# Three buffers instead of four for the expert tiles' inputs and outputs, in a two-layer transformer kernel

## What is computed

```python
x = x + _L0_attn_ref(_layernorm(x, axis=-1), ...)
x = x + _L0_ffn_ref(_layernorm(x, axis=-1), ...)
x = x + _L1_attn_ref(_layernorm(x, axis=-1), ...)
x = x + _L1_ffn_ref(_layernorm(x, axis=-1), ...)
```

## Time and profile before

| what | value |
|---|---|
| time, median of 3 runs | 3438.32 us (3438.31 to 3441.68) |
| the profiled execution's own time | 3441.68 us |
| its span, first to last instruction | 3439.8 us |
| expert stage, first load to last scatter issued | 1376.5 to 1598.2 us |
| busy over the whole span | PE 90%, DVE 73%, ACT 67%, POOL 45% |
| mean granted TensorE clock | 0.945 |

### The profile page before, as it was taken

How to read it: one execution, slowest core, us unless ns; L and a number is a source line. 1 busy time by engine, 2 the same in 40 slices (tenths; PEclk the granted TensorE clock), 3 DMA queues, 4 the chain that set the end, 5 groups by cost and what they waited for, 6 DMA issues and landing times. The chain is left out here.

```text
span 3439.8 us, 73149 instructions
## 1 busy us (share of the span) xinstructions
PE 3110.3 (90%) x22770; PEld 1708.7 (50%) x22770; DVE 2501.7 (73%) x7023; ACT 2299.8 (67%) x3127; POOL 1533.6 (45%) x1807
## 2 busy tenths in 40 slices
PE   6999996799999885994499999999999999999979
PEld 2555553455555553883244444444444444444456
DVE  4666654888888872664688888888888888888754
ACT  4877772465655553443688888888888888888722
POOL 3454442345555534576434444444444444444433
PEclk8999996899999997997699999999999999999989
DMA  4444542322222212563200000000000000000001
GB/s 102 117 107 102 118 115 61 73 57 58 61 64 66 65 43 48 170 175 110 58 0 4 6 2 7 0 9 0 9 0 3 6 0 9 0 9 0 0 16 34
DMA packets 173144, 162.18 MB, mean 47 GB/s; under 512 B 18276, under 2 KB 156735, under 8 KB 172830
## 3 DMA queue, kind: packets, MB, share of 16 engines
q1 hardware_dynamic: 163838, 142.35, 17.1%
q0 software_dynamic: 9088, 16.88, 1.5%
HBM read 92.40 MB, written 68.52 MB: 47 GB/s over the span
## 5 line engine op out<-in xcount | busy, mean ns | idle before, releaser
L2759 POOL TENSOR_TENSOR lb_y<-lb_ao,XC 128x512 f32<-128x512 f32 x128 | 163.1, 1274 | 801.7 <-ACT lb_ao L2706 801.7
L2598 PE MATMUL lb_H<-lb_x,lb_w 128*128 (+1 forms) x1024 | 513.7, 604 | 0.5 <-issue 0.5
L547 ACT ACTIVATE ga_PT<-ga_S 128x1024 f32<-128x1024 f32 (+1 forms) x384 | 336.6, 881 | 262.7 <-PE ga_S L374 262.4
L2607 PE MATMUL lb_FF<-lb_h,lb_w 128*128 128x512 f32 x1024 | 460.3, 592 | 0.0
L2713 ACT ACTIVATE lb_h<-lb_H,lb_prm 128x512 f32<-128x512 f32 x512 | 351.7, 687 | 99.4 <-PE lb_H L2598 84.4
L2805 DVE TENSOR_SCALAR lb_z<-lb_M,lb_mv,lb_rstd 128x128 f32<-128x128 f32 x1024 | 349.9, 404 | 32.9 <-POOL lb_rstd L2750 27.7
L2607 PEld LDWEIGHTS lb_FF<-lb_h,lb_w 128*128 128x128 f32 x1024 | 194.6, 190 | 244.9 <-issue 215.4
L2750 POOL TENSOR_TENSOR lb_rstd<-lb_rstd,half 128x4 f32<-128x4 f32 x256 | 259.2, 1012 | 36.9 <-issue 0.2
L2797 DVE BATCH_NORM_STATS2 lb_stats<-lb_M 128x6 f32<-128x128 f32 x1024 | 228.3, 286 | 29.5 <-PE lb_M L2580 18.0
L2598 PEld LDWEIGHTS lb_H<-lb_x,lb_w 128*128 128x128 f32 x1024 | 174.0, 190 | 132.2 <-issue 122.8
L1522 POOL TENSOR_SCALAR_AFFINE_SELECT da_PT<-da_PT 128x1024 f32<-128x1024 f32 x128 | 145.9, 1145 | 201.1 <-ACT da_PT L1452 201.1
(11 more groups left out here) (335 smaller groups left out, 7185.9 us busy)
## 6 DMA issues: line engine op xcount, KB each, us to landing
moe_w<-experts_dram SPq DMA_DIRECT2D x39, 384.0 KB, 3.3
da_qT<-da_stq SPq DMA_DIRECT2D x64, 192.0 KB, 4.2
da_kT<-da_stk SPq DMA_DIRECT2D x64, 192.0 KB, 5.1
ga_qT<-ga_stq SPq DMA_DIRECT2D x32, 384.0 KB, 6.1
moe_x<-moe_xs SPq DMA_DIRECT2D x39, 258.0 KB, 3.7
tc_g<-moe_ys SPq DMA_DIRECT2D x32, 256.0 KB, 3.5
da_stq<-da_parts SPq DMA_DIRECT2D x16, 384.0 KB, 2.4
da_stk<-da_parts SPq DMA_DIRECT2D x16, 384.0 KB, 3.0
```

The lines of the kernel that those rows point to most:

```text
L547: act.activation(PT[:, n % RING, :, lo:hi], score_banks(u)[:, :, 0:hi - lo], ACT.Exp, scale=SCALE).then_inc(probs, 1)
L2598: pe.matmul(H[:, k % 2, :], w1[:, k, :], x1_of(i), start=True, stop=True).then_inc(h_filled, 1)
L2607: pe.matmul(FF[:, :], w2[:, k, :], h[:, k, :], start=(k == 0), stop=(k == KC - 1)).then_inc(ff_filled, 1)
```

## The change

The counts of buffers XR (for x and w) and YR (for y and the destinations) go from 4 to 3. All else follows from these two numbers: how many tiles are loaded at the start, which tile a load has to wait for, how far `address` may run ahead of the scatters, and the size of the four tensors.

```diff
@@ -1783,8 +1783,8 @@
 
     F = 256
     FC = F // P
-    XR = 4
-    YR = 4
+    XR = 3
+    YR = 3
 
     own = []
     with ExitStack() as ctx:
```

## The result

| | median of the runs | runs |
|---|---|---|
| before | 3440.0 us | 4, 3438.31 to 3442.75 |
| changed | 3535.9 us | 4, 3532.49 to 3541.84 |
| ratio | 1.028 | 95% interval 1.0262 to 1.0298 |

The changed kernel is 95.9 us slower; the prediction said 99.9 us and 3538 us.

The account below looks back on a forecast made before the run. The prediction took the w load's undivided round trip of 8.0 us as the period, replacing POOL's 5.2 us a tile; 36 trips plus the end made the stage 99.9 us longer: 3438.3 + 99.9 = 3538 us, range 3518 to 3566.

Parts of the forecast that it names:

- The bound: Expert stage: POOL's 5.2 us a tile sets the end before; with three buffers the w load's undivided round trip does.
- which take releases which load: w(j+XR) is issued after take(j); its round trip has two periods with four buffers, one with three.
- The trip: From take through w load and copy_w to the next take: 1.43 + 3.3 + 3.23 = 7.96 us, taken as 8.0.
- the sum of 99.9: Expert stage's end: 36 round trips of 8.0 us, then POOL's last tiles, ending at 1698.1 instead of 1598.17.
- The estimate of 2.9 us for the load: Alternative price for the 384 KB w load from the skill's fit: period 7.6 us, 3524 us in all.
- YR costs nothing: In address, waiting for scatters of tile j-3: 7.9 us against two periods of 16 us, so no wait, no cost.
- TensorE is early: In each tile TensorE finishes 3.9 us before its down is wanted and idles 3.0 us.
- the clock rival: TensorE's clock falls to 0.50 throughout, period 10.0 us, 72 us more, 3610 us; chance 0.06.
- ACT's wait: ACT's wait for w ahead of copy_w: some 5.7 us a tile, about 205 us in all instead of 65.9.
- The end: Stage's end: POOL finishes three tiles 19.6 us after copy_w(38); last scatter starts about 10 us behind last take.
- The start: Stage's start: take(0) stays at 1393.76; dropping the fourth tile's initial loads changes nothing.
- POOL's waits: POOL's scatters wait for take about 2.8 us a tile, some 100 us in all.

Follow-up runs that it names:

- x3y4: The changed kernel with YR back at 4 (XR = 3): 3538.48 us against 3445.72 us of the kernel before beside it, ratio 1.0266.
- down_gate: The changed kernel (XR = YR = 3) with the w load waiting for the tile's down matmuls instead of the copy behind them: 3469.05 us, ratio 1.0065 to the kernel before.
- split3: The changed kernel with w in two loads, gate and up released after rest_of_w, down as in the changed kernel: 3446.32 us, ratio 1.0004 to the kernel before.
- dbl3: The changed kernel (XR = YR = 3) with every later w load done twice, the second after the first has landed: 3683.23 us.
- dbl4: The kernel before (XR = YR = 4) with every later w load done twice, run two times: 1.0020 and 1.0004 of the kernel before beside it.
- x4y3: The kernel before with YR = 3 and XR still 4: 3442.85 us, ratio 0.9997 to the kernel before.
- base_again: The kernel before, unchanged, run and profiled again on another chip: 3530.78 us.
- x5y4: The kernel before with a fifth input buffer (XR = 5, YR = 4): ratio 1.0003, beside a kernel before of 3529.82 us.
- split3b: split3 with the gate and up load issued one tile further ahead, run two times: 1.0024 and 1.0016 of the kernel before beside it.

## Why the prediction was right

- *The bound, and which take releases which load.* Right, and shown: x3y4 puts the loss on XR, down_gate and split3 take three quarters and all of it back through the release of the load alone, and dbl3 against dbl4 shows the trip paid once a tile with three buffers and covered with four.
- *The trip.* Worked out 7.96 us, rounded to 8.0; measured 7.88 on average in the changed kernel and 7.90 in x3y4. In the trip shown above 1.43 to the issue was 1.43, and 3.23 from copy_w to take was 3.20; if these hold for the others, the load's mean is what is left of 7.88, 3.25 where I took 3.3. The rounding and the load together are 36 x 0.12 = 4.3 us, and the sum of 99.9 is 4.0 above the measured 95.9.
- The estimate of 2.9 us for the load from the fit in the Trainium skill ("DMA: Bandwidth & Descriptors", Anatomy of one DMA) would have given 3524 us, below all timed runs; the row of this queue was the better price.
- *YR costs nothing.* Right for the time (x4y3). Wrong in a detail: alone, beside XR = 4, it does make address wait, 54.1 us. I had compared the trip with two whole periods, and left out that VectorE, ahead of POOL, runs into the ring whatever its length. The wait takes the place of POOL's backlog and is free.
- *TensorE is early and the clock rival.* TensorE idles 2.6 us in the tile shown and (50 - 36.44) / 50 x 7.9 = 2.1 a tile on average (I had 3.0). The clock was not at 1.00 as I had expected. Windows of the changed kernel:

```profile
1422.00:1470.00 48.00, 35.63 (x198) 29.17 (x197) 19.31 (x36) 13.08 (x24) 26.48 (x26) 0.93 0.39 118
...
1520.00:1570.00 50.00, 36.44 (x197) 30.04 (x198) 21.64 (x41) 13.80 (x26) 24.83 (x25) 0.92 0.35 106
```

  It dips and comes back. The burst at 1520.82 begins at a granted clock of 1.00 after 2.61 us of idle time; the clock is 0.50 from 1522 to 1524 and 1.00 again from 1525, and the first four matmuls are busy for 1.53 us in place of 1.17. A mean of 0.92 costs nothing, since TensorE has 3.9 us to spare, as said. The Trainium skill ("TensorE: Matmul & The Clock Gate", HAM oscillation) describes a kernel in which every burst behind a DMA wait starts low. Here most bursts run at 1.00 throughout, and in the one shown the fall comes after its start.
- *ACT's wait.* Forecast about 205 us, measured 232.3; I had left out its wait for the first tile, 26.7 us before and 25.6 after. POOL's waits: about 100 forecast, 125.3 - 27.3 = 98.
- *The end.* From the start of take(36) to the end of the last scatter 16.3 us by my sum, 16.6 measured. Two errors nearly cancel in it, which is luck: from take to its first scatter the sum has 1.0 us, and it is 1.57 in the earlier trace rows (1393.76 to 1395.33) and 1.51 at 1703.37; and twelve scatters take 15.1 us, where the sum has 15.3. The last scatter starts 8.3 us behind the last take (9.9 in x3y4), where I had said about 10. The start: take(0) stands 17.3 us behind the first load before and 17.4 after.

## What to carry to other kernels

A ring of n buffers gives a load's round trip fewer periods than n. Subtract those that the consumer's own order uses up, here two: going from four to three halved the cover instead of taking a quarter. Add the whole trip up, from the release through the issue and the landing to the next release, and divide it by that number; as long as it is below the slowest engine's pace a buffer less costs nothing, and beyond that each microsecond is paid on every tile. Before buying a buffer, look at what releases it: a release at the last reader, or two loads for parts that are read last at different times, gave back three quarters and all of the loss with three buffers. And a wait that grows (address in x4y3, ACT in split3) is no loss where the engine that sets the pace is still fed.

## What the runs showed of the hardware that was not expected

The same kernel took 3440 us beside some runs and 3531 us beside others, each steady to about 0.4%. The profiles of the second kind in which the load of w does not set the pace (base_again, x5y4, dbl4, split3b) have idle times of ACT and DVE ("remote", "issue"; up to 5.4 us in base_again) that no instruction of the program explains. Most of them lie in the expert stage, which took 280.1 us in place of 221.7. The two kinds went with the chip in these runs; that it is the chip, and not something else that differed between the times of the runs, was not tested. What these engines wait for was not found. That w or x land later does not explain it: in x5y4 the waits for both (29.1 us of ACT for w, 26.8 us of TensorE for x) were those of the start alone, and the stage took 288.2 us. What can be said is that the loss by a change depends on it: 96 us on the one, 39 on the other.
